# A selective scan's product with C moved between the half scans of the next group

## The chip, the cores and the metric

The kernel runs on one core of one Trainium2 chip. The metric is the device time of one execution in microseconds (us). The engines are TensorE (PE in the rows; PEld is its weight load), VectorE (DVE), ScalarE (ACT), GpSimd (POOL) and SyncE (SP, which issues the DMAs). Each runs its own instructions in order and waits on semaphores for the others.

## What is computed

The input x is 32 images of 14 x 14 positions and 384 channels. A gated recurrent layer over the 196 positions is added to it, and then a selective scan block. The change touches only the second, whose core is

```
dts = softplus(dt_proj(x_dbl) + bias)            # per direction k (4), channel d (192), position t
h   = h * exp(dts[t] * A[n]) + dts[t] * u[t] * B[n, t]      # state n of 16
y   = sum over n of h[n, t] * C[n, t]            # + D * u
```

scanned over t = 0..195 in four directions (rows, columns, and both backwards). The four results are summed, normalised over the channels, multiplied by silu(z) and projected back.

## The kernel before

The scan part goes over 16 pairs of images (`pair`, the first and the last written out, the 14 between in a loop), in each over four stages `st` (the directions), in each over twelve groups `g`. A group is four sequences of 196 positions on 128 partitions (784 columns) of one or more states; 16 x 4 x 12 = 768 groups. Its tile is one of six buffers, `hb`. For each group:

- POOL (`drive`, L495) writes dt * u * B into `hb`. It waits until the group six back has been summed.
- ACT (`decays`, L980 for groups 0 to 7, L984, two instructions a half, for 8 to 11) writes exp(dt * A) of each half group into one of three PSUM banks (`DEC`). The decay of a half waits for the half scan three back.
- DVE (`scan`, L786 forwards, L789 backwards) runs two half scans in place in `hb`, 392 columns each, and then (`read_out`, L798) multiplies the whole tile by C, which lies spread over the partitions in two PSUM banks.
- PE (`spread`, L1258) writes C of the next group into these banks when the product has been made (`readout_ready`), and then (`reduce`, L1268) adds the tile with an identity matrix to the sums in banks 5 and 6.

Between these, at fixed groups, the queues hold the rest. PE has the projections for the next stages, and for the pair before the centring, variance and out-projection (L1283 to L1289, L1316 to L1323). ACT has the softplus of the next stage, the copies of the sums out of banks 5 and 6 (`drain`, L996, at stages 0 and 2), and for the pair before the copies of the centred values (L1002, stage 0, groups 6 and 8), the logarithm of the variance (L1025, stage 1, groups 6 and 8), an affine step (L1013, stage 2, group 2) and the copies of the result (L1019, stage 2 group 8, stage 3 groups 6 and 8). ACT does these after the decays of the group named. PE makes the values for them in stage 0 at groups 4, 5 and 7, in stage 1 at 5 and 7, in stage 2 at 6, in stage 3 at 4 and 6, each after the sum of the group before. Before the sum of the first group of stages 0 and 2, PE waits for the copies of `drain` (L1340 to L1343), because this sum starts the banks anew.

Of the kernel before, what the change touches and what calls it, by code (L numbers as in the profile page):

```python
# [27 lines left out]
PAIRS = B // 2  # L28
# [3 lines left out]
K4 = 4  # L32
T2 = 2 * T
TC = 3 * T
GRP = 12
# [14 lines left out]
def build(nc, x_seq, x_pair, wx, wh, bx, bh, wp, win, par, xproj, dtproj, wout, out):  # L50
# [6 lines left out]
    with ExitStack() as ctx:  # L57
# [3 lines left out]
        def sem(name):  # L61
            return ctx.enter_context(nc.semaphore(name))
# [71 lines left out]
        def carve(cols):  # L134
# [29 lines left out]
        s = {n: sem(n) for n in (  # L164

            "params_in", "gru_weights_in", "late_weights_in", "dt_w_clear", "xload0", "xload1", "xload2", "xload3",

            "ident0", "ident_ready", "sel_step", "gavg_step", "const_ready", "pad_zero", "d_zero", "setup_step",
            "a_exp", "a_capped", "bias_step", "bcw_step", "centring_step", "skip_step",

            "st_done", "a_gn", "a_g1", "a_g2", "a_std", "a_rstd",

# [35 lines left out]
        def group_aps(g):  # L208

            if g < 8:  # L210
                return (lambda a: a[:, 0:T2].unsqueeze(1).broadcast_to([128, 2, T2]),
                        lambda bank: ps[:, bank:bank + 2, 0:T2],
                        lambda a: a.rearrange("p (m c) -> p m c", m=2))
            return (lambda a: a[:, T2:TC].unsqueeze(1).unsqueeze(1).broadcast_to([128, 2, 2, T]),
                    lambda bank: ps[:, bank:bank + 2, 0:T2].rearrange("p m (q t) -> p m q t", q=2),
                    lambda a: a.rearrange("p (m q t) -> p m q t", m=2, q=2))

        def half_cols(hf):

            return slice(hf * HALF_C, (hf + 1) * HALF_C)  # L220
# [323 lines left out]
        def _(dve):  # L544
# [232 lines left out]
            def scan(st, g, hf, G):  # L777

                q = (st * GRP + g) % RING
                bank = (2 * (st * GRP + g) + hf) % DEC  # L780
                if hf == 0:
                    dve.wait_ge(s["drive_ready"], G + 1)
                dve.wait_ge(s["decay_ready"], G * 2 + (hf + 1))
                h = hb[q][:, half_cols(hf)]
                if KS[st] < 2:
                    dve.tensor_tensor_scan(h, ps[:, bank, 0:HALF_C], h, 0.0, ALU.mult, ALU.add  # L786
                        ).then_inc(s["scan_done"], 1)
                else:
                    dve.tensor_tensor_scan(h[:, ::-1], ps[:, bank, 1:HALF_C + 1][:, ::-1], h[:, ::-1], 0.0, ALU.mult, ALU.add  # L789
                                           ).then_inc(s["scan_done"], 1)  # L790

            def read_out(st, g, G):

                _, bank, view = group_aps(g)
                h = view(hb[(st * GRP + g) % RING])
                dve.wait_ge(s["scan_done"], G * 2 + 2)
                dve.wait_ge(s["c_ready"], G + 1)
                dve.tensor_tensor(h, h, bank(3), ALU.mult).then_inc(s["readout_ready"], 1)  # L798

            def pair(i, head, last):  # L800
                for st in range(K4):
                    for g in range(GRP):
                        G = i * (K4 * GRP) + (st * GRP + g)
                        for hf in range(2):
                            scan(st, g, hf, G)
                        read_out(st, g, G)

            pair(0, True, False)
            with nc.Fori(1, PAIRS - 1, engines=[dve.engine], hint_back_edge=True) as i:
                pair(i, False, False)  # L810
            pair(PAIRS - 1, False, True)


        @block.scalar
        def _(act):
# [123 lines left out]
            def mid_parts(P, st):  # L939
                act.wait_ge(s["resid_ready"], P + 1)  # L940
                act.activation(bcs[st][32:64, :], resid[32:64, :], ACT.Copy).then_inc(s["mid_ready"], 1)
                act.activation(midt[64:96, :], resid[64:96, :], ACT.Copy).then_inc(s["mid_ready"], 1)
# [24 lines left out]
            def decays(P, st, g, hf, H, early=False):  # L967

                k, b = KS[st], st % 2
                bank = (2 * (st * GRP + g) + hf) % DEC  # L970
                lo = 1 if k < 2 else 0
                r = ps[:, bank, 0:HALF_C].rearrange("p (r t) -> p r t", t=T)[:, :, 1:T]
                if (g, hf) == (0, 0):
                    act.wait_ge(s["delta_ready"], P + 1)
                if not early:
                    act.wait_ge(s["scan_done"], H - (DEC - 1))
                if g < 8:
                    src = delta[b][:, 0:T2].rearrange("p (r t) -> p r t", r=2)[:, :, lo:lo + T - 1]
                    c = k * N + 2 * g + hf
                    ins = act.activation(r, src, ACT.Exp, scale=a01[:, c:c + 1], bias=abias01[:, c:c + 1])  # L980
                else:
                    for m in range(2):
                        c = k * N + 4 * (g - 8) + 2 * hf + m
                        ins = act.activation(r[:, m, :], delta[b][:, T2 + lo:T2 + lo + T - 1], ACT.Exp,  # L984
                                             scale=a2[:, c:c + 1], bias=abias2[:, c:c + 1])
                ins.then_inc(s["decay_ready"], 1)

            def drain(i, end):

                act.wait_ge(s["reduced"], i * (K4 * GRP) + (48 if end else 24))  # L990
                for dst, bank, rows in (((y_wh if end else y_hw)[:, 0:T2], 5, 2), ((y_wh if end else y_hw)[:, T2:TC], 6, 1)):
                    src = ps[:, bank, 0:rows * T]
                    if end:
                        dst = dst.rearrange("p (r h w) -> p r h w", h=H, w=W)
                        src = src.rearrange("p (r w h) -> p r h w", w=W, h=H)
                    act.activation(dst, src, ACT.Copy).then_inc(s["y_drained"], 1)  # L996
# [7 lines left out]
            def square(i):  # L1004

                act.wait_ge(s["yc_ready"], i * 2 + 2)
                act.activation(ysq, yc, ACT.Square).then_inc(s["ysq_ready"], 1)
# [24 lines left out]
            def pair(i, head, last):  # L1032
                for st in range(K4):
                    P1, n1, k1 = i * 4 + (st + 1), (st + 1) % K4, KS[(st + 1) % K4]
                    ahead = not (last and st == K4 - 1)
                    for g in range(GRP):
                        for hf in range(2):
                            H = i * (2 * K4 * GRP) + (2 * (st * GRP + g) + hf)
                            if not (head and 2 * (st * GRP + g) + hf < DEC):
                                decays(i * 4 + st, st, g, hf, H)  # L1040
                        if g == 1:
                            if st == 0 and not head:
                                drain(i - 1, True)
                            if st == 2:
                                drain(i, False)
                        if ahead:
                            if g == 2:
                                softplus(P1, k1, 0)
                            if g == 3:
                                mid_parts(P1, n1)  # L1050
                            if g == 4:
                                softplus(P1, k1, 1)
                            if g == 5:
                                series(P1, 0)
                            if g == 6:
                                series(P1, 1)
                        if not head:
                            if (st, g) in ((0, 6), (0, 8)):
                                centred(i - 1, g // 2 - 3)
                            if (st, g) == (0, 9):  # L1060
                                square(i - 1)
                            if (st, g) in ((1, 6), (1, 8)):
                                log_var(i - 1, g // 2 - 3)
                            if (st, g) == (1, 9):
                                rstd(i - 1)
                            if (st, g) == (2, 2):
                                affine(i - 1)
                            if (st, g) in ((2, 8), (3, 6), (3, 8)):
                                result(i - 1, (g // 2 - 2) if st == 3 else 0)
                        if (st, g) == (3, 7) and not last:  # L1070
                            act.wait_ge(s["du_ready"], i * 4 + 4)
                            turn(i + 1)
                        if g == 11 and not (last and st >= 2):
                            read_bc(i * 4 + (st + 2), (st + 2) % K4)
# [392 lines left out]
```

## Time and profile before

| | us |
|---|---|
| median of three runs | 3129.97 (3129.74 to 3130.99) |
| the profiled execution | 3124.29, span 3122.5 |
| DVE busy | 2624.9 (84%) |
| PE busy | 2718.1 (87%) |
| POOL busy | 2142.9 (69%) |
| ACT busy | 1812.7 (58%) |

The recurrent layer fills the first third of the span, then come the input projections and the convolution; the scan part runs from about 967 us to 3092 us, with a tail of 30 us. In the rows the first number of a timeline is the start in us from the start of the span, the second how long it lasts, x2 how many instructions are merged in the row; in brackets stands how long the engine was idle before, and who ended that.

### The profile page before, as it was taken

The numbers are of one execution on the slowest core, as the hardware profiler recorded it, in microseconds if no ns is written. First come the engines' busy times: TensorE is split into PE (matmuls) and PEld (weight loads), VectorE is DVE, ScalarE is ACT, GpSimd is POOL, SyncE is SP. The second block draws the span as 40 slices with busy tenths as digits, with TensorE's granted clock in tenths as the row PEclk, the third lists the DMA queues.
The fourth block names the chain that finished last, engine by engine and source line by source line (L and its number), as shares of the span: only waits on it lengthen the run. The fifth ranks groups of instructions, "written<-read, shape, count | busy, mean of one in ns | idle before, by whom it ended". The sixth has DMA issues, their size and how long they took to land.

```text
span 3122.5 us, 100405 instructions
## 1 busy us (share of the span) xinstructions
PE 2718.1 (87%) x39088; PEld 2026.1 (65%) x39088; DVE 2624.9 (84%) x4163; ACT 1812.7 (58%) x3812; POOL 2142.9 (69%) x1816
## 2 busy tenths in 40 slices
PE   4999999999996788888888888888888888888886
PEld 3999999996654465665655656556566656656554
DVE  6444444445999999999999999999999999999995
ACT  1111111112226777777777777777777777777774
POOL 5333333331006888988889888988989889888883
PEclk9999999999998999999999999999999999999999
DMA  5000000002335455454554555555555555545541
GB/s 207 0 0 0 0 0 0 0 0 82 139 133 176 139 164 179 142 177 145 168 165 149 165 159 164 161 168 156 158 168 151 163 165 150 180 144 172 173 125 48
DMA packets 57087, 385.30 MB, mean 123 GB/s; under 512 B 10100, under 2 KB 15060, under 8 KB 31700
## 3 DMA queue, kind: packets, MB, share of 16 engines
q1 hardware_dynamic: 57044, 384.79, 39.8%
q8 instruction: 20, 0.33, 0.0%
q14 instruction: 23, 0.19, 0.0%
HBM read 352.64 MB, written 32.11 MB: 123 GB/s over the span
## 4 chain that ended last, share of the span: by engine, by line
POOL 35%; issue 28%; PE 26%; DVE 8%; ACT 1%; POOLq 1%; DMA 0%; DVEq 0%; ACTq 0%
POOL arena L495 22%; PE ps L1138 10%; PE ps L1147 10%; PE ps L1179 3%; POOL arena L468 3%; POOL arena L477 3%; POOL arena L482 3%; POOL arena L472 3%; DVE arena L789 2%; DVE arena L786 2%; PE ps L1134 2%; DVE conv_out L202 1%; POOL arena L460 1%; DVE stats L571 1%; POOL arena L455 1%
## 5 line engine op out<-in xcount | busy, mean ns | idle before, releaser
L1268 PE MATMUL ps<-arena,ident 128*128 128x392 f32 (+1 forms) x4096 | 1164.3, 417 | 0.9 <-DVE arena L798 0.9
L980 ACT ACTIVATE ps<-arena,abias,a 128x390 f32<-128x390 f32 x1024 | 688.7, 677 | 306.0 <-DVE arena L789 177.0
L1268 PEld LDWEIGHTS ps<-arena,ident 128*128 128x128 f32 x4096 | 683.3, 191 | 144.3 <-issue 1.3
L798 DVE TENSOR_TENSOR arena<-arena,ps 128x784 f32<-128x784 f32 x768 | 745.6, 971 | 28.0 <-PE ps L1258 1.8
L786 DVE TENSOR_TENSOR_SCAN arena<-ps,arena 128x392 f32<-128x392 f32 x768 | 702.7, 956 | 7.5 <-issue 4.4
L789 DVE TENSOR_TENSOR_SCAN arena<-ps,arena 128x392 f32<-128x392 f32 x768 | 702.7, 957 | 0.0
L1258 PE MATMUL ps<-arena,sel 96*128 96x196 bf16 x3072 | 391.7, 250 | 307.9 <-DVE arena L798 307.4
L1258 PEld LDWEIGHTS ps<-arena,sel 96*128 96x128 bf16 x3072 | 230.4, 98 | 612.4 <-DVE arena L798 578.0
L495 POOL TENSOR_TENSOR arena<-arena 128x784 f32<-128x784 f32 x256 | 474.2, 1852 | 133.2 <-PE ps L1268 130.8
L984 ACT ACTIVATE ps<-arena,abias,a 128x195 f32<-128x195 f32 x1024 | 474.6, 504 | 136.3 <-DVE arena L786 69.3
L495 POOL TENSOR_TENSOR arena<-arena,wh_sb 128x784 f32<-128x784 f32 x256 | 472.7, 1852 | 71.8 <-PE ps L1268 69.7
L495 POOL TENSOR_TENSOR arena<-arena,wx_sb 128x784 f32<-128x784 f32 x256 | 466.6, 1856 | 19.5 <-POOL arena L482 15.1
L426 POOL COPY arena<-h_t 128x96 f32 x196 | 71.9, 367 | 407.5 <-DVE h_t L673 407.5
L1138 PE MATMUL ps<-wx_sb,x_cur 128*32 128x96 f32 x14112 | 333.2, 248 | 0.0
L1147 PE MATMUL ps<-wh_sb,h_t 128*32 128x96 f32 x14112 | 332.9, 247 | 0.0
L658 DVE TENSOR_TENSOR rh<-r_gate,ps 128x96 f32<-128x96 f32 x196 | 49.8, 254 | 313.3 <-PE ps L1147 313.3
L1138 PEld LDWEIGHTS ps<-wx_sb,x_cur 128*32 128x32 f32 x14112 | 290.9, 110 | 23.1 <-issue 0.2
L1147 PEld LDWEIGHTS ps<-wh_sb,h_t 128*32 128x32 f32 x14112 | 299.2, 110 | 7.4
L844 ACT ACTIVATE r_gate<-ps 128x96 f32<-128x96 f32 x196 | 49.2, 251 | 399.2 <-PE ps L1147 399.2
L1237 PE MATMUL ps<-arena,bc_w 128*128 128x196 f32 x768 | 149.5, 332 | 2.6 <-DVE gsum L732 2.6
L443 POOL TENSOR_TENSOR grstd<-gsum,neg_half 128x2 f32<-128x2 f32 x16 | 13.5, 844 | 199.3 <-DVE gsum L732 199.3
L1237 PEld LDWEIGHTS ps<-arena,bc_w 128*128 128x128 f32 x768 | 133.2, 192 | 20.2 <-issue 3.0
(180 smaller groups left out, 3025.9 us busy)
## 6 DMA issues: line engine op xcount, KB each, us to landing
wx_sb<-b_by_state SPq DMA_DIRECT2D x64, 1568.0 KB, 6.3
wh_sb<-b_by_state SPq DMA_DIRECT2D x64, 1568.0 KB, 6.3
arena<-b_by_image SPq DMA_DIRECT2D x128, 784.0 KB, 9.0
arena<-x_seq SPq DMA_DIRECT2D x4, 2352.0 KB, 16.1
x_in<-x_pair SPq DMA_DIRECT2D x16, 588.0 KB, 4.2
x_dram<-x SPq DMA_DIRECT2D x16, 588.0 KB, 3.1
x<-x_dram SPq DMA_DIRECT2D x16, 588.0 KB, 10.0
out<-xhat SPq DMA_DIRECT2D x16, 588.0 KB, 2.9
```

Of the source, the lines that this page charges most:

```text
L468: pool.tensor_tensor(rest, soft, rest, ALU.subtract).then_inc(s["rest_ready"], 1)
L495: pool.tensor_tensor(view(hb[(st * GRP + g) % RING]), dux(du[b]), view(src), ALU.mult).then_inc(s["drive_ready"], 1)
L786: dve.tensor_tensor_scan(h, ps[:, bank, 0:HALF_C], h, 0.0, ALU.mult, ALU.add).then_inc(s["scan_done"], 1)
L789: dve.tensor_tensor_scan(h[:, ::-1], ps[:, bank, 1:HALF_C + 1][:, ::-1], h[:, ::-1], 0.0, ALU.mult, ALU.add).then_inc(s["scan_done"], 1)
L798: dve.tensor_tensor(h, h, bank(3), ALU.mult).then_inc(s["readout_ready"], 1)
L980: ins = act.activation(r, src, ACT.Exp, scale=a01[:, c:c + 1], bias=abias01[:, c:c + 1])
L984: ins = act.activation(r[:, m, :], delta[b][:, T2 + lo:T2 + lo + T - 1], ACT.Exp, scale=a2[:, c:c + 1], bias=abias2[:, c:c + 1])
L1138: mm = pe.matmul(ps[32 * j:32 * j + 32, bank + p, 0:CJ], x_cur[:, p, 32 * k:32 * k + 32], wx_sb[:, k, j, lo:lo + CJ], start=False, stop=False)
L1147: mm = pe.matmul(ps[32 * j:32 * j + 32, bank + p, at:at + CJ], h_t[:, 1 - p, 32 * k:32 * k + 32], wh_sb[:, k, j, lo:lo + CJ], start=False, ...
L1237: mm = pe.matmul(ps[:, 7, bc * T:(bc + 1) * T], bc_w[:, k, bc, tile, :], x[:, tile * T:(tile + 1) * T], start=(tile == 0), stop=(tile == 2))
L1258: mm = pe.matmul(ps[:, 3 + m // 2, m % 2 * T:m % 2 * T + T], sel[:, n, kind, :], rhs, start=True, stop=True)
L1268: mm = pe.matmul(ps[:, 5 if g < 8 else 6, 0:cols], ident[:, :], h[:, m * cols:(m + 1) * cols], start=(opens and m == 0), stop=(closes and ...
```

## The change

The product of a group is issued after the first half scan of the next group, so that DVE's order is first half scan of g, product of g-1, second half scan of g. The last product of all stands behind the last pair. It waits for `2 * done` half scans and `done` spreads of C, where `done` is the count of groups before g. On ACT, the copies of the sums (`drain`) go from behind the decays of group 1 to behind those of group 2, in stages 0 and 2. The number of instructions of each engine stays the same.

```diff
-            def read_out(st, g, G):
+            def read_out(st, g, done):
 
                 _, bank, view = group_aps(g)
                 h = view(hb[(st * GRP + g) % RING])
-                dve.wait_ge(s["scan_done"], G * 2 + 2)
-                dve.wait_ge(s["c_ready"], G + 1)
+                dve.wait_ge(s["scan_done"], done * 2)
+                dve.wait_ge(s["c_ready"], done)
                 dve.tensor_tensor(h, h, bank(3), ALU.mult).then_inc(s["readout_ready"], 1)
 
             def pair(i, head, last):
                 for st in range(K4):
                     for g in range(GRP):
                         G = i * (K4 * GRP) + (st * GRP + g)
-                        for hf in range(2):
-                            scan(st, g, hf, G)
-                        read_out(st, g, G)
+                        scan(st, g, 0, G)
+                        if not (head and (st, g) == (0, 0)):
+                            read_out(*((st, g - 1) if g else ((st - 1) % K4, GRP - 1)), G)
+                        scan(st, g, 1, G)
...
             pair(PAIRS - 1, False, True)
+            read_out(K4 - 1, GRP - 1, PAIRS * K4 * GRP)
...
-                        if g == 1:
+                        if g == 2:
                             if st == 0 and not head:
                                 drain(i - 1, True)
                             if st == 2:
```

## Rows read from the trace of the kernel before

**Rows 1.** Costliest groups of the page: busy and mean ns of one; idle before.

```profile
L798 DVE TENSOR_TENSOR arena<-arena,ps 128x784 f32<-128x784 f32 x768 | 745.6, 971 | 28.0 <-PE ps L1258 1.8
L786 DVE TENSOR_TENSOR_SCAN arena<-ps,arena 128x392 f32<-128x392 f32 x768 | 702.7, 956 | 7.5 <-issue 4.4
L789 DVE TENSOR_TENSOR_SCAN arena<-ps,arena 128x392 f32<-128x392 f32 x768 | 702.7, 957 | 0.0
```

**Rows 2.** Windows view, one pair: length; busy PE, PEld, DVE, ACT, POOL; clock, DMA.

```profile
1497.20:1629.30 132.10, 113.86 (x584) 79.81 (x584) 130.46 (x145) 100.11 (x192) 117.37 (x75) 1.00 0.52 160
```

**Rows 3.** Timeline of DVE in that pair, stages 0, 1 and 2.

```profile
1499.09 0.97 DVE L798 TENSOR_TENSOR arena<-arena,ps 128x784 f32<-128x784 f32 x1
1499.98 1.83 DVE L786 TENSOR_TENSOR_SCAN arena<-ps,arena 128x392 f32<-128x392 f32 x2
...
1507.34 0.97 DVE L798 TENSOR_TENSOR arena<-arena,ps 128x784 f32<-128x784 f32 x1
...
1515.60 0.97 DVE L798 TENSOR_TENSOR arena<-arena,ps 128x784 f32<-128x784 f32 x1
...
1530.25 1.83 DVE L789 TENSOR_TENSOR_SCAN arena<-ps,arena 128x392 f32<-128x392 f32 x2
...
1543.12 0.97 DVE L798 TENSOR_TENSOR arena<-arena,ps 128x784 f32<-128x784 f32 x1
...
1548.62 0.97 DVE L798 TENSOR_TENSOR arena<-arena,ps 128x784 f32<-128x784 f32 x1
...
1578.90 0.97 DVE L798 TENSOR_TENSOR arena<-arena,ps 128x784 f32<-128x784 f32 x1
```

**Rows 4.** Timeline of ACT, stage 0, groups 6 to 9.

```profile
1514.60 0.50 ACT L1002 ACTIVATE arena<-ps 128x392 f32<-128x392 f32 x1 [0.59 <-PE ps L1285]
1514.99 1.27 ACT L980 ACTIVATE ps<-arena,abias,a 128x390 f32<-128x390 f32 x2
...
1520.51 0.34 ACT L1002 ACTIVATE arena<-ps 128x196 f32<-128x196 f32 x1 [2.07 <-PE ps L1289]
1520.74 1.82 ACT L984 ACTIVATE ps<-arena,abias,a 128x195 f32<-128x195 f32 x4
```

**Rows 5.** Timeline of PE, stage 0, the spread for group 7.

```profile
1516.63 0.51 PE L1258 MATMUL ps<-arena,sel 96*128 96x196 bf16 x4 [0.39 <-DVE arena L798]
```

**Rows 6.** Timeline of ACT, stage 1, groups 6 to 9.

```profile
1547.36 0.50 ACT L1025 ACTIVATE arena<-ps 128x392 f32<-128x392 f32 x1 [0.33 <-PE ps L1285]
1547.76 1.27 ACT L980 ACTIVATE ps<-arena,abias,a 128x390 f32<-128x390 f32 x2
...
1552.54 0.34 ACT L1025 ACTIVATE arena<-ps 128x196 f32<-128x196 f32 x1 [1.07 <-PE ps L1289]
1552.77 1.82 ACT L984 ACTIVATE ps<-arena,abias,a 128x195 f32<-128x195 f32 x4
```

**Rows 7.** Timeline of ACT, stage 2, groups 1 to 3.

```profile
1565.32 0.72 ACT L996 ACTIVATE arena<-ps 128x392 f32<-128x392 f32 x2 [0.36 <-PE ps L1268]
...
1567.03 0.68 ACT L980 ACTIVATE ps<-arena,abias,a 128x390 f32<-128x390 f32 x1 [0.42 <-DVE arena L786]
...
1569.64 1.27 ACT L980 ACTIVATE ps<-arena,abias,a 128x390 f32<-128x390 f32 x2
```

**Rows 8.** Timeline of all engines at the start of the last pair.

```profile
2961.04 1.28 ACT L980 ACTIVATE ps<-arena,abias,a 128x390 f32<-128x390 f32 x2
...
2961.82 1.84 DVE L786 TENSOR_TENSOR_SCAN arena<-ps,arena 128x392 f32<-128x392 f32 x2 [3.05 <-ACT ps L980]
```

**Rows 9.** Timeline of PE, stage 2: a spread, the out-projection's last.

```profile
1563.41 0.51 PE L1258 MATMUL ps<-arena,sel 96*128 96x196 bf16 x4 [0.89 <-DVE arena L798]
...
1582.94 0.82 PE L1323 MATMUL ps<-x,ident 128*128 128x392 f32 x2
```

**Rows 10.** Timeline of POOL, stage 0: group 10, then the next stage's groups.

```profile
1513.32 1.86 POOL L495 TENSOR_TENSOR arena<-arena 128x784 f32<-128x784 f32 x1 [1.16 <-PE ps L1268]
...
1523.18 7.29 POOL L495 TENSOR_TENSOR arena<-arena,wx_sb 128x784 f32<-128x784 f32 x4 [0.24 <-POOL arena L482]
```

## What the change should do to the time

> **What bounds the kernel now.** I read the costliest groups of instructions first, then the busy time of each engine over one pair of images, then the timelines of VectorE (DVE), ScalarE (ACT) and TensorE (PE). The last 2120 us are 768 groups, each two half scans (L786 or L789) and one product with C (L798) on DVE [rows 1]. Over the 48 groups of the pair from 1497.2 to 1629.3, DVE is busy 130.46 of 132.10 us and no other engine comes near; PE's clock is 1.00, that is 2.4 GHz [rows 2]. So DVE sets the end, and what counts is the distance between the starts of its instructions. One group takes 132.10 / 48 = 2.752 us; its busy time is 130.46 / 48 = 2.718, so 0.034 us is idle.
>
> The durations overlap: 0.956 + 0.957 + 0.971 = 2.884 us [rows 1] against 2.718 covered, so 0.166 us is covered twice. In [rows 3] the product starts at 1499.09 and the next scan at 1499.98, 0.89 later, though the product lasts 0.97; two scans together span 1.83. These two starts overlap what stands before them by 0.166 / 2 = 0.083 us. The third, from the second half scan to the product of the same group, doesn't: the product reads what that scan wrote, waits for its end and starts 0.034 after it. In start-to-start distances: product to scan 0.888, scan to scan 0.873, scan to its own product 2.752 - 0.888 - 0.873 = 0.991.
>
> **What the change removes.** The product of group g-1 now follows the first half scan of g, and what it waits for ended a whole instruction earlier. It should start like any other, 0.873 after the scan ahead of it. The trace has no scan followed by a product that is free to start; the nearest rows are scan to scan and product to scan. A group then takes 0.873 + 0.888 + 0.873 = 2.634 us, 0.118 less, and 768 x 0.118 = 90.6 us is the gain. Its lower bound is the idle time alone, 768 x 0.034 = 26 us, or nothing; I see no reason for more than 0.118. I take 0.118, because both kinds of neighbour in the trace that wait for no DVE result overlap alike.
>
> The Trainium skill ("VectorE: DVE Perf Modes", "The DRAIN you can't avoid") speaks against this: it says that the next operation can't start until the pipe is empty, that a semaphore after each operation costs nothing extra, and in its rules for authors to save operations, not semaphores. The trace's 0.991 against 0.873 is after a wait on DVE's own result and without one. By the page the sum would have no gain term; this is the third rival.
>
> **What it costs: PE's work slides against ACT's.** PE starts group g+1 (C's spread, L1258, then the sum of group g, L1268, then whatever stands behind) when product g is done. ACT's decays (L980, L984) go by the scans. The product now ends one scan later relative to the scans, so wherever ACT waits in its queue for PE, the decays behind that copy come later, and the next scan needs them. ACT has such waits at four places of each pair but the first, at the norm of the pair before: L1002 in stage 0 (groups 6 and 8) and L1025 in stage 1 (groups 6 and 8). Each holds the first decays of group 7 or 9.
>
> I take the length of each chain from the start of the product that releases PE to the end of the decay, plus 0.10 from an ACT end to DVE's start (the decay from 2961.04 ends at about 2961.72, the scan starts at 2961.82) [rows 8]:
> - Stage 0, group 9. Product 6 starts 1515.60 [rows 3], PE's spread 1516.63 [rows 5], the copy 1520.51, the decays 1520.74, two of them done at +0.94 [rows 4]: 1521.68 - 1515.60 + 0.10 = 6.18 us.
> - Stage 0, group 7. Product 3 at 1507.34, copy at 1514.60 after the centring in two groups, decay from 1514.99 (+0.68): 8.43 us [rows 3, 4].
> - Stage 1, group 7. Product 4 at 1543.12, decay from 1547.76 (+0.68): 5.42 us [rows 3, 6].
> - Stage 1, group 9. Product 6 at 1548.62, decays from 1552.77 (+0.94): 5.19 us [rows 3, 6].
>
> The time that DVE gives them was 2 x 2.752 + 0.888 = 6.39 us from product g to the first scan of g+3 (one group more, 9.14, for the second). All four fitted, the first with 0.2 to spare, and DVE doesn't stop there. After the change the product stands behind the first half scan of the next group: the distance is 2 x 2.634 - 0.873 = 4.40 us, or 7.03 with a group more. The stalls are 6.18 - 4.40 = 1.78, 8.43 - 7.03 = 1.40, 5.42 - 4.40 = 1.02 and 5.19 - 4.40 = 0.79, in sum 4.99 us a pair. They add up, since each chain starts from a product behind the stall before it. Fifteen pairs have them: 75 us. With 0.1 us more or less in each of the four, 69 to 81.
>
> **The moved copies** (L996, at stages 0 and 2). They wait for the sum of the last group of the stage before, which also comes a scan later; at group 1 ACT would stand before them, at group 2 it needn't. They start at 1565.32, 1.91 after the spread at 1563.41 [rows 7, 9]; by the new distances that is 3.8 us into the stage, and ACT is through with the decays of group 2 at 4.3. Moved, they stand between the decays of groups 2 and 3. In stage 2, the fullest, ACT goes without rest from the decay at 1567.03 to that of group 3 at 1569.64 [rows 7]. With 0.72 for the copies, and 0.06 from a DVE end to the start that it releases (product 6 ends at 1516.57, the spread starts at 1516.63): 0.06 + 2.61 + 0.72 + 0.68 + 0.10 = 4.17 us, against 2 x 2.634 - 0.956 = 4.31 that DVE gives. It fits by 0.14; nothing is lost, and if it didn't fit, 0.1 us would be lost once a pair. PE waits for them ahead of the sum of the stage's first group (L1343), perhaps 0.2 us; only the spread of group 2 is behind, and between two products it has 2.634 - 0.971 - 0.06 - 0.51 - 0.10 = 1.0 us to spare. No DMA moves.
>
> **Others.** The out-projection's copies (L1019) stand one group further behind PE: product 5 at 1578.90, last matmul from 1582.94 (+0.82) [rows 3, 9]; with 0.50 for the copy (as L1002's of the same shape), 0.94 and 0.10 that is 6.4 us against 7.03. No stall, cover 0.6. GpSimd (POOL) waits for the sum of group 4 before its drive of group 10 [rows 10]. Product g stands at 1.87 + 2.752g of a stage, and at 3.51 + 2.634g after the change, 1.2 us later for group 4, and POOL's work behind it as well. Its drives for the next stage start at 1523.18, 7.29 / 4 = 1.82 each: the first is done 5.2 us before its scan at 1530.25 [rows 3]. That leaves 5.2 - 1.2 - 12 x 0.118 = 2.6 us: covered. The last product stands at the end of the queue as before; the tail doesn't change.
>
> **Sum.** -90.6 + 75 = -15.7 us. The profiled execution took 3124.29 us (span 3122.5), so it would be 3108.6; the median of the runs shown is 3129.97, 5.7 more, and from it the forecast is 3114.3.
>
> **Rivals.**
> 1. *The stalls outweigh the gain* (slower). The point from which it decides is 90.6 / 15 = 6.04 us a pair, one more than my sum. It comes where a cover that I call sufficient isn't: 0.1 at the moved copies, 0.6 at the out-projection's copies, or PE a little later at the four. For it: the covers are small and ACT is busy 100.11 of 132.10 us [rows 2]. With 6.8 us a pair it is +11 us, 3141 us. Against it: the chains are measured whole, not put together. Chance 0.15.
> 2. *The chains are shorter than counted*, because a part of PE's work that I hang on the product can run before it. With 3 us a pair: 3130 - 90.6 + 45 = 3084 us. For it: group 7 of stage 0 hangs on three groups of PE's queue. Against it: the spread stands first in each group of that queue and waits for the product. Chance 0.14.
> 3. *DVE starts no product until the scan before it has ended.* Then the change doesn't do what it says. If only the 0.034 goes, a group takes 2.718, the distances are 4.48 and 7.20, the stalls 4.58 a pair: 3130 - 26 + 69 = 3173 us, chance 0.06. If nothing goes: distances 2 x 2.752 - 0.991 = 4.51 and 7.27, stalls 4.42: 3130 + 66 = 3196 us, chance 0.03. Against both: the 0.083 at the other two starts.
>
> **How the numbers follow.** Forecast 3114 us, chance 0.62, its own range 3102 to 3129 (stalls 69 to 81, gain per group 0.113 to 0.120, and 5 us either way for the last pair, where DVE stands 3.05 us for ACT [rows 8]). Range for 8 in 10: from rival 2 to rival 1, 3084 to 3141; left out are 0.09 of rival 3 and tails. A measurement here can tell some 0.2% from nothing, 6.3 us: faster below 3123.7. Of the forecast's 0.62 some 0.53 lies there, with rival 2 0.67; 0.12 within; 0.21 slower, from rivals 1 and 3.
>
> **What will show it.** The start distances on DVE: first half scan to product 0.87 (rival 3: 0.96 or more), a group in stages 2 and 3 at 2.63 us, 31.6 us for twelve. DVE's idle time before a scan with ACT's L980 and L984 as releasers, some 75 us in all, 1.4 and 1.8 us at groups 7 and 9 of stage 0, 1.0 and 0.8 in stage 1; none in the first pair. ACT's waits for PE at L1002 and L1025 grow by about 2 us each. Stalls at group 3, or in stages 2 and 3, would mean that a cover failed (rival 1). The prediction is wrong if stages 0 and 1 take as long as 2 and 3.

## The result, and the profile after

The changed kernel takes 3090.62 us (median; 3084.21 to 3094.28), the kernel before beside it 3130.48 us: a ratio of 0.987 (95% interval 0.9853 to 0.9887), 39.9 us faster. The forecast was 3114.3 us. The time lies inside the stated range and on the forecast side, but below the forecast's own range of 3102 to 3129, and the gain is 2.5 times the 15.7 us that the sum gave. The profiled execution took 3084.21 us, 40.1 less than that of before, so the two profiles show the whole difference.

The costliest groups of the page after, which answer [rows 1] (busy and mean ns of one, then idle before and its main releaser):

```profile
L786 DVE TENSOR_TENSOR_SCAN arena<-ps,arena 128x392 f32<-128x392 f32 x768 | 708.9, 958 | 44.6 <-ACT ps L986 24.9
L789 DVE TENSOR_TENSOR_SCAN arena<-ps,arena 128x392 f32<-128x392 f32 x768 | 708.8, 958 | 23.3 <-ACT ps L982 13.3
L798 DVE TENSOR_TENSOR arena<-arena,ps 128x784 f32<-128x784 f32 x768 | 727.2, 947 | 1.0 <-PE ps L1260 0.6
```

The 28.0 us that DVE idled in front of products are 1.0; in front of scans it idles 67.9 us, released by ACT's decays (L982 and L986 are the lines L980 and L984 of before). The product itself is shorter, 947 ns against 971. The timeline of DVE in stage 0 of a pair, groups 6 to 9, which answers [rows 3]:

```profile
1501.71 0.97 DVE L786 TENSOR_TENSOR_SCAN arena<-ps,arena 128x392 f32<-128x392 f32 x1 [1.28 <-ACT ps L982]
1502.60 0.94 DVE L798 TENSOR_TENSOR arena<-arena,ps 128x784 f32<-128x784 f32 x1
1503.47 1.83 DVE L786 TENSOR_TENSOR_SCAN arena<-ps,arena 128x392 f32<-128x392 f32 x2
1505.21 0.94 DVE L798 TENSOR_TENSOR arena<-arena,ps 128x784 f32<-128x784 f32 x1
1506.08 0.97 DVE L786 TENSOR_TENSOR_SCAN arena<-ps,arena 128x392 f32<-128x392 f32 x1
1508.70 0.97 DVE L786 TENSOR_TENSOR_SCAN arena<-ps,arena 128x392 f32<-128x392 f32 x1 [1.66 <-ACT ps L986]
1509.59 0.94 DVE L798 TENSOR_TENSOR arena<-arena,ps 128x784 f32<-128x784 f32 x1
```

A group without a stall goes from product to product in 1505.21 - 1502.60 = 2.61 us: product to scan 0.87 (1502.60 to 1503.47), two scans to the next product 1.74. In medians over all groups of the two traces, the three distances between starts went so: from a product to the scan behind it 0.888 before and 0.863 after, from that scan to the next one 0.883 and 0.883, from the second scan to the product 0.981 and 0.865. ACT in the same stretch, which answers [rows 4]:

```profile
1500.61 0.50 ACT L1004 ACTIVATE arena<-ps 128x392 f32<-128x392 f32 x1 [2.47 <-PE ps L1287]
1501.01 1.27 ACT L982 ACTIVATE ps<-arena,abias,a 128x390 f32<-128x390 f32 x2
...
1507.49 0.34 ACT L1004 ACTIVATE arena<-ps 128x196 f32<-128x196 f32 x1 [3.45 <-PE ps L1291]
1507.72 1.82 ACT L986 ACTIVATE ps<-arena,abias,a 128x195 f32<-128x195 f32 x4
```

ACT waits 2.47 and 3.45 us for PE where it waited 0.59 and 2.07; the decays behind each copy release the stalled scans. In the rows of DVE a stall shows as 1.28 and 1.66 us of idle time, but it costs 1.38 and 1.77: the scan also lasts 0.97 us where one right behind another scan lasts 0.95, and it can't overlap what stands ahead.

**Where the 40.1 us are.** Times go from product start to product start. The last row is what the others leave over; in it, the stretch ahead of the first scan, on which the change has no part, took 965.1 us after and 967.5 before.

| | before | after | difference, us |
|---|---|---|---|
| a group without a stall | 2.752 | 2.610 | 768 x -0.142 = -109.1 |
| pair in the loop, 48 groups | 132.11 | 130.52 | |
| of it over 48 groups at that rate (stalls) | 0 | 5.24 | 15 x 5.24 = +78.6 |
| what the first 12 groups of the last pair take over those of a loop pair | 8.1 | 0.5 | -7.6 |
| rest (ahead of the scans, first pair, tail) | | | -2 |

### The profile page after: what moved, and what is told of

Its sections match the earlier page's. It is cut to its first block, busy times and chain, and to the rows that moved or that the text cites. A ratio compares the mean times of both kernels' runs of the same rounds, so it can differ in the third digit from the quotient of the medians.

```text
span 3082.4 us, 100405 instructions
## 1 busy us (share of the span) xinstructions
PE 2710.2 (88%) x39088; PEld 2029.7 (66%) x39088; DVE 2553.4 (83%) x4163; ACT 1813.3 (59%) x3812; POOL 2143.2 (70%) x1816
## 4 chain that ended last, share of the span: by engine, by line
POOL 36%; PE 28%; issue 26%; DVE 8%; ACT 1%; POOLq 1%; DMA 0%; DVEq 0%; ACTq 0%
POOL arena L495 22%; PE ps L1140 10%; PE ps L1149 10%; PE ps L1181 3%; POOL arena L468 3%; POOL arena L472 3%; POOL arena L477 3%; POOL arena L482 3%; PE ps L1136 2%; DVE arena L789 1%; DVE arena L786 1%; DVE arena L798 1%; POOL arena L460 1%; DVE conv_out L202 1%; POOL arena L455 1%
## 5 line engine op out<-in xcount | busy, mean ns | idle before, releaser
L1270 PE MATMUL ps<-arena,ident 128*128 128x392 f32 (+1 forms) x4096 | 1164.1, 417 | 0.0
L982 ACT ACTIVATE ps<-arena,abias,a 128x390 f32<-128x390 f32 x1024 | 684.6, 678 | 208.3 <-DVE arena L789 109.8
L1270 PEld LDWEIGHTS ps<-arena,ident 128*128 128x128 f32 x4096 | 681.6, 190 | 149.5 <-ACT arena L998 6.5
L798 DVE TENSOR_TENSOR arena<-arena,ps 128x784 f32<-128x784 f32 x768 | 727.2, 947 | 1.0 <-PE ps L1260 0.6
L1260 PEld LDWEIGHTS ps<-arena,sel 96*128 96x128 bf16 x3072 | 237.9, 97 | 566.8 <-DVE arena L798 529.3
L986 ACT ACTIVATE ps<-arena,abias,a 128x195 f32<-128x195 f32 x1024 | 465.9, 503 | 54.5 <-DVE arena L786 34.1
L495 POOL TENSOR_TENSOR arena<-arena,wx_sb 128x784 f32<-128x784 f32 x256 | 467.2, 1854 | 24.8 <-PE ps L1270 15.7
```

Of the source, the lines that this page charges most:

```text
L495: pool.tensor_tensor(view(hb[(st * GRP + g) % RING]), dux(du[b]), view(src), ALU.mult).then_inc(s["drive_ready"], 1)
L1260: mm = pe.matmul(ps[:, 3 + m // 2, m % 2 * T:m % 2 * T + T], sel[:, n, kind, :], rhs, start=True, stop=True)
L1270: mm = pe.matmul(ps[:, 5 if g < 8 else 6, 0:cols], ident[:, :], h[:, m * cols:(m + 1) * cols], start=(opens and m == 0), stop=(closes and ...
```

## The experiments

The theory after the result: a DVE instruction that waits for the end of the one right ahead of it pays 0.142 us for that, not the 0.118 of the forecast, and the stalls come from ACT's queue order as forecast. Rivals: the product is faster by where it stands; the stalls are a lack of time that would only move; the moved copies carry a part of the gain. Each kernel below was timed beside the kernel before, on the same chip as the others of its group.

### The two parts alone

Only the moved copies, in the old order:

```diff
-                        if g == 1:
+                        if g == 2:
                             if st == 0 and not head:
                                 drain(i - 1, True)
```

> The old order on DVE, only the copies of the sums (drain) moved on ACT from group 1 to group 2. Theory (all of the gain comes from DVE's order): the same time as before, within 3 us; a group stays at 2.752 us, no idle time of DVE in front of a scan in the loop. Rival (the moved copies carry a part of the gain that the rate of the scans doesn't explain): faster by 5 us or more.

Measured: 3153.53 us against 3130.14, ratio 1.007 (1.0054 to 1.0087), 23 us slower. Neither theory had this. The waits of the kernel (in all, times, longest), the timeline of PE at the start of one stage 0, and a row from the stage 2 behind it:

```profile
DVE arena L798 <- PE ps L1258: 23.5, 28, 1.5
PE ps L1268 <- ACT arena L996: 53.4, 31, 1.7
```

```profile
1510.40 0.51 PE L1258 MATMUL ps<-arena,sel 96*128 96x196 bf16 x4 [0.23 <-DVE arena L798]
...
1512.64 2.44 PE L1268 MATMUL ps<-arena,ident 128*128 128x392 f32 x4 [1.72 <-ACT arena L996]
1514.87 0.86 PE L1258 MATMUL ps<-arena,sel 96*128 96x196 bf16 x4
...
1579.79 1.58 PE L1268 MATMUL ps<-arena,ident 128*128 128x392 f32 x4 [1.72 <-ACT arena L996]
```

PE stands 1.72 us for the copies before it may start the banks anew, and then, in the first of the two stages, runs for the most part at the lower of its two clocks: the sum takes 2.44 us where it took 1.51, the spread of C 0.86 for 0.51. The windows view (length; busy PE, PEld, DVE, ACT, POOL; granted clock, DMA share, GB/s) has 0.61 of full speed for that stretch, a mean of times at 1.2 and at 2.4 GHz, and 1.00 before it:

```profile
1508.00:1512.60 4.60, 2.68 (x16) 1.82 (x14) 4.53 (x6) 2.70 (x6) 4.50 (x4) 1.00 0.45 174
1512.60:1515.40 2.80, 2.76 (x8) 1.46 (x9) 2.25 (x3) 2.75 (x6) 0.25 (x1) 0.61 0.95 390
```

The product of group 2 then waits 0.98 us for C. The trace tells the wait from the clock, since PE stands the same 1.72 us at all 31 of these places. Behind 13 of them, as at 1579.79, the sum took 1.58 or 1.59 us and the products lost 0.01 us or nothing. Behind the other 18 PE ran slowly (the sum 1.90 to 2.98 us) and the products lost 1.06 to 1.46 us each, but for one that lies among the gaps of the last pair: in sum some 20 of the 23 us. So in the old order the late copies do harm, not by PE's wait itself, but by the clock that falls behind some of the waits.

Only the new order of DVE, the copies left at group 1 (the last hunk of the change undone):

> The new order on DVE with the copies of the sums left at group 1. ACT then stands at group 1 until the sum of the last group of the stage before, about 3.8 us into the stage. Theory: in stage 2, where softplus and the affine step follow, the decay of group 3 is done 8.4 us into the stage and the scan wants it at 7.83: 0.6 us of DVE idle once a pair, 9 us in all, about 3099 us. Rival (the place of the copies doesn't matter): 3090 us, no idle time at group 3.

Measured: 3097.03 us, ratio 0.9894 (0.9877 to 0.991), as expected within 2 us. The stall is in front of the scan of group 3 in stage 2, as expected, and 0.38 us long where 0.6 was worked out:

```profile
1563.44 0.97 DVE L786 TENSOR_TENSOR_SCAN arena<-ps,arena 128x392 f32<-128x392 f32 x1 [0.38 <-ACT ps L982]
```

The order alone is worth 33 us. The copies give another 6.4 on top of it, and cost 23 without it: the two parts belong together.

### What a wait for the instruction ahead costs

The changed kernel, where the product waits for one half scan more, the one right ahead of it, which it doesn't read (`own` is 1, and 0 for the very last product):

```diff
-                dve.wait_ge(s["scan_done"], done * 2)
+                dve.wait_ge(s["scan_done"], done * 2 + own)
```

> The new order, but the product also waits for the half scan right ahead of it, whose result it doesn't read. Theory A (a DVE instruction that waits for the end of the one ahead pays for it, wherever it stands: 0.034 idle, 0.083 of overlap, and 0.024 by which it lasts longer itself): product 0.971 long again, a group 2.752 us, the four stalls 4.4 us a pair: about 3130 + 66 = 3196 us, less some 7 if the last pair's gap stays away. Theory B (the product is short because of where it stands beside PE's work): product 0.945, a group 2.728 or less, under 3180 us.

Measured: 3183.63 us against 3130.14, ratio 1.0169 (1.0152 to 1.0186), 93 us slower than the changed kernel by one wait. The timeline of DVE:

```profile
1567.19 0.97 DVE L798 TENSOR_TENSOR arena<-arena,ps 128x784 f32<-128x784 f32 x1
1568.07 1.83 DVE L789 TENSOR_TENSOR_SCAN arena<-ps,arena 128x392 f32<-128x392 f32 x2
1569.94 0.97 DVE L798 TENSOR_TENSOR arena<-arena,ps 128x784 f32<-128x784 f32 x1
```

The product is 0.97 long again and a group takes 2.75 us, in the new place. That is theory A. The stalls of a loop pair are 136.39 - 132.11 = 4.28 us, the third rival's second case gave 4.42 for this rate. So 768 waits cost 109 us at 0.142 each, and some 14 of them come back as smaller stalls (4.28 us a pair for 5.24); the total of 3183.63 is 5 us under the 3189 that theory A gave without the last pair's gap. The same wait for another engine does the same to the length: 16 products of the changed kernel waited for C until 0.02 us after the end of the scan ahead, and they last 0.971 too.

The product behind both half scans of the next group, so that it waits for nothing near, with ACT's norm steps moved as in the next section:

```diff
                         scan(st, g, 0, G)
+                        scan(st, g, 1, G)
                         if not (head and (st, g) == (0, 0)):
                             read_out(*((st, g - 1) if g else ((st - 1) % K4, GRP - 1)), G)
-                        scan(st, g, 1, G)
```

> As e4 (ACT's norm steps one group later), but the product of the group before stands behind both half scans of the next group, not between them. It waits for no DVE result that isn't long there. Theory (what counts is that the product doesn't wait for the instruction ahead; the place is free): product 0.945 us, a group 2.610 us in stages without a stall, as between the halves. The product comes 0.87 us later, so PE's chains end later: from product 6 to the scan of group 10 there are 6.1 us against 6.2, at the out-projection 6.1 against 6.4; some 1 us a pair of stalls, 3040 us. Rival (it must stand between the halves, since two scans side by side and the product behind them cost more): a group over 2.65 us, over 3060 us.

Measured: 3038.74 us against 3129.11, ratio 0.9713 (0.9697 to 0.973). Its rate is the same:

```profile
1576.67 0.94 DVE L798 TENSOR_TENSOR arena<-arena,ps 128x784 f32<-128x784 f32 x1
1577.54 1.83 DVE L789 TENSOR_TENSOR_SCAN arena<-ps,arena 128x392 f32<-128x392 f32 x2
1579.29 0.94 DVE L798 TENSOR_TENSOR arena<-arena,ps 128x784 f32<-128x784 f32 x1
```

So the place between the half scans isn't what matters for the rate; it is only the earliest one that doesn't wait. The later place costs 15.5 us against the next kernel, which has the product between the halves. A pair takes 126.87 us, 0.94 more, about the 1 us that was expected, but not where it was expected: the scan that idles is that of group 3 in stage 2, 0.64 us each time.

### Where the stalls come from

The changed kernel, ACT's copies of the centred values and the logarithms (and the square and rstd behind them) one group later:

```diff
-                            if (st, g) in ((0, 6), (0, 8)):
+                            if (st, g) in ((0, 7), (0, 9)):
                                 centred(i - 1, g // 2 - 3)
-                            if (st, g) == (0, 9):
+                            if (st, g) == (0, 10):
                                 square(i - 1)
-                            if (st, g) in ((1, 6), (1, 8)):
+                            if (st, g) in ((1, 7), (1, 9)):
                                 log_var(i - 1, g // 2 - 3)
-                            if (st, g) == (1, 9):
+                            if (st, g) == (1, 10):
                                 rstd(i - 1)
```

> The new order, and on ACT the copies of the centred values, their square, the logarithms of the variance and the rstd one group later (stage 0 at groups 7, 9, 10; stage 1 the same). Theory (the four stalls a pair come from the decays that stand behind these copies in ACT's queue): the idle time of DVE in front of scans goes from about 68 us to under 5, a pair in the loop takes 125.5 us instead of 130.5, the total is 3090 - 73 = 3017 us. Rival (the stalls are a lack of time on ACT or PE and only move): the idle time comes back at groups 8 and 10, and the total stays over 3070 us.

Measured: 3023.22 us (3022.80 to 3027.33) against 3130.14, ratio 0.9661 (0.9645 to 0.9677). This version beats both kernels, the changed one by 67 us, and is 6 us behind what was expected. The groups of its page and a window of its scan part:

```profile
L786 DVE TENSOR_TENSOR_SCAN arena<-ps,arena 128x392 f32<-128x392 f32 x768 | 709.8, 967 | 0.4 <-ACT ps L982 0.4
L789 DVE TENSOR_TENSOR_SCAN arena<-ps,arena 128x392 f32<-128x392 f32 x768 | 708.1, 963 | 0.0
```

```profile
1497.20:1629.30 132.10, 119.29 (x623) 85.94 (x622) 132.08 (x152) 105.02 (x202) 122.89 (x79) 1.00 0.57 169
```

Of the 67.9 us of idle in front of scans 0.4 is left, and DVE is busy 132.08 of 132.10 us. A pair takes 125.93 us, not 125.5; that is the 6 us. What it has over 48 x 2.610 = 125.28 are mostly steps of 2.68 to 2.71 us at groups where the product comes just behind C.

Stage 0's steps alone, stage 1 left:

> The changed kernel with only stage 0's norm steps of ACT one group later; stage 1's logarithms stay. Theory (each stall belongs to its own copy, and they add up): stage 0 loses its 1.39 + 1.77 us, stage 1 keeps 1.00 + 0.77: 3090 - 15 x 3.0 = 3045 us. Rival (the stalls are one lack that moves on): stage 1's stalls grow, the total stays over 3060 us.

Measured: 3046.23 us, ratio 0.974 (0.9724 to 0.9756). In stage 1 the distances from product to product stay 3.60 and 3.38 us, as in the changed kernel. The stalls belong each to its own copy.

The same move of ACT's steps in the old order:

> The old order on DVE (copies of the sums at group 1, as before), and only ACT's copies of the centred values, the square, the logarithms and the rstd one group later. In the old order these stop no scan. Theory (moving them gives back stalls of the new order, and nothing else): the same as before, 3130 us within 3. Rival (their early place costs something in the old order too): faster by 5 us or more. Second reading: the last pair's gap on DVE in front of the scan of group 9 of stage 0, 4.4 us in the profile of before and not there in any kernel with the new order; if the old order's code brings it, it is here again.

Measured: 3128.75 us against 3129.11, ratio 1.0001 (0.9991 to 1.001). By itself it does nothing: the old order has no such stalls, and a pair in its loop takes 132.1 us with the move and without it.

### PE standing before the sums

The changed kernel with the copies of the sums at group 3 (`g == 3` for `g == 2`):

> The changed kernel with the copies of the sums one group later still, at group 3. PE then stands before the sum of group 0 until they are through, from 4.9 to about 7.6 us into stages 0 and 2, as it stood 1.7 us in the old order with the copies at group 2. The spread of C for group 2 comes behind that sum, and the product of group 2 would start at 8.7. Theory A (PE's granted clock falls after it has stood, so that the sum takes 2.4 us and not 1.35, as in the old order): the product of group 2 starts 1.9 us late, twice a pair, 60 us in all, about 3150 us, and the windows view shows a clock well under 1.00 there. Theory B (PE only stood, at its full clock): 0.85 us late, 27 us, about 3117 us.

Measured: 3178.94 us against 3130.22, ratio 1.0156 (1.0139 to 1.0173). Its waits, and one stage 0:

```profile
DVE arena L798 <- PE ps L1260: 84.2, 51, 3.4
PE ps L1270 <- ACT arena L998: 93.2, 31, 3.5
```

```profile
1514.85 2.36 PE L1270 MATMUL ps<-arena,ident 128*128 128x392 f32 x4 [2.59 <-ACT arena L998]
1585.60 1.58 PE L1270 MATMUL ps<-arena,ident 128*128 128x392 f32 x4 [3.40 <-ACT arena L998]
```

In the first row PE stood 2.59 us and ran slowly behind it (granted clock 0.69 from 1514 to 1518), in the second it stood 3.40 us and the sum went at nearly full speed. Of the 31 places of this kind 24 are slow behind the wait (the sum takes 1.91 to 2.98 us) and 7, all in stage 2, are not (1.58 or 1.59). The products lose 2.3 to 4.3 us at each of the 24, and 1.7 or 1.8 at each of the 7. So both theories have a part: the clock falls at most of the places, as theory A has it, but the wait alone costs 1.7 us where PE stood 3.4, twice what theory B gave it. Together they make 88 us where theory A had 60. What decides whether the clock falls, neither this run nor the one with the old order tells. In the changed kernel the matmuls of the sums have no idle time ahead of them at all (0.0 in the page's group L1270).

### The last pair's gaps

DVE stands twice in front of a scan at the start of the last pair of the kernel before, and once more, 0.5 us, in front of a product. The waits of DVE there ("issue": nothing that the profile shows), of before and then of the changed kernel:

```profile
DVE arena L786 <- issue: 4.4, 1, 4.4
DVE arena L786 <- ACT ps L980: 3.1, 1, 3.1
```

```profile
DVE arena L786 <- ACT ps L982: 1.7, 2, 1.3
DVE arena L786 <- ACT ps L986: 1.7, 1, 1.7
```

Of these rows of the changed kernel only 0.4 us is the gap of before, the rest are the known stalls. Three kernels asked whether the place of the instructions decides. The first was meant to put eight waits ahead of DVE's scan part:

> The kernel before with eight waits on a value long reached, on DVE ahead of the scan part: they take nothing worth measuring, but every DVE instruction behind them lies eight places further on. Theory A (the last pair's gap in front of group 9, 4.4 us without a waited-for event, comes from where the instructions lie): it moves to another group or goes, and the time may fall by up to 5 us. Theory B (it comes from the order of the work or the traffic at that moment): the gap stays in front of group 9 of stage 0 with 4 us or more, and the time is that of before.

Measured: 3128.27 us against 3129.11, ratio 1.0004 (0.9994 to 1.0013), with a gap of 7.7 us in front of group 9. The waits moved the code by fewer places than was meant. Three semaphore instructions of the new line stand in the trace, and a fourth at L782; they hold one or two waits each, and the rest hang on instructions that were there. The first lines of the two pages, of before and of this run, differ by those four:

```profile
span 3122.5 us, 100405 instructions
span 3125.6 us, 100409 instructions
```

So four places further on, the gap is still in front of group 9. The next two use small memsets, one in the new order (shown) and 16 in the old:

```diff
+            for n in range(1):
+                dve.memset(gru_bias[:, n:n + 1], 0.0).then_inc(s["const_ready"], 1)
             pair(0, True, False)
```

> The changed kernel with one small memset more on DVE ahead of the scan part. In the changed kernel the first pair has one instruction less than before, so that DVE's loop and last pair lie one place earlier; the memset puts them back to the places they have in the kernel before. Theory A (the last pair's gap of 4 to 7 us on DVE in front of the scan of group 9 hangs on where the instructions lie): the gap is there again, and the median is 3095 us or more. Theory B (it hangs on the order): no gap in front of group 9, 3090.6 us within 3.

> The kernel before with 16 small memsets more on DVE ahead of the scan part (1 to 2 us by themselves), so that its loop and last pair lie 16 places further. Theory A (place): the gap in the last pair moves to another group or goes; where it goes the time is 3130 + 2 - 6 = 3126 us. Theory B (order): the gap stays in front of group 9, 3132 us.

Measured: 3091.08 us for the new order (the changed kernel: 3090.62), with no gap in front of group 9; 3127.63 us against 3131.13 for the old, ratio 0.9992 (0.9982 to 1.0001), where the gap in front of group 9 is gone and one of 1.74 us stands in front of group 7:

```profile
2975.87 1.27 ACT L982 ACTIVATE ps<-arena,abias,a 128x390 f32<-128x390 f32 x2
...
2977.08 0.94 ACT L986 ACTIVATE ps<-arena,abias,a 128x195 f32<-128x195 f32 x2
...
2978.61 1.84 DVE L786 TENSOR_TENSOR_SCAN arena<-ps,arena 128x392 f32<-128x392 f32 x2 [1.74 <-ACT ps L986]
```

The releaser named can't be the true one: L986 (L984 of before) makes group 8's decays, and those of group 7, L982 here, end at 2977.14, 1.5 us before the scan. It is a gap of the same kind, two groups earlier.

Counting all of DVE's instructions in the trace, those of its sequencer too, the gap stands in front of number 8124 in the kernel before (and in those with the moved copies and with ACT's steps later), of 8128 with the eight waits and of 8130 with the 16 memsets. In the old order it keeps to nearly the same place in the code, whatever the group, 1.7 to 7.7 us long. The new order shows none, with or without the memset, but the old place isn't quite met there: by the same count its last pair begins four instructions earlier than before, and three earlier with the memset. The kernel with the product behind both half scans has a small one, 0.9 us, in front of number 8122 and of group 9. So the place decides where the gap stands, and the order has a part in whether there is one.

The trace also has the packets that load instruction code, as a kind of their own. From 1200 to 2940 us, within the loop, the kernel before has none. Its last pair is straight code that runs for the first time, and in the first 50 us of it there are seven. One of them lies in the gap of DVE, between 2980.4 and 2981.2 us. In the run with the 16 memsets one lies in the gap in front of group 7, between 2976.8 and 2977.2. The DMA view of these two windows (queue and kind, packets, MB, share of 16 engines; the data packets have the first row):

```profile
q1 hardware_dynamic: 16, 0.20, 125.6%
q14 instruction: 1, 0.01, 5.0%
```

```profile
q14 instruction: 1, 0.01, 5.3%
```

In all six programs with such a gap (the five of the old order and the one with the product behind both half scans) a packet of code ends 1.3 to 1.7 us before DVE goes on. ACT's stop at the start of the last pair, 5.2 us in the kernel before and 1.7 in the changed one, has one too, and ACT goes on 1.2 and 1.3 us after its end. In the changed kernel the packet ends 26.5 us after the loop, and the scan of group 9, in front of which the gap would stand, starts at 29.6; in the kernel before it ends at 31.5, and DVE has stood since 28.8. So the likely cause is that the engine waits for its code. It is not shown: the trace doesn't say whose code a packet holds. Why the packet comes 5 us later in one order than in the other stays open; while DVE stood in the kernel before, data packets filled the DMA engines (the first fence), and in the short gap with the 16 memsets there were none.

## Why the prediction was wrong in size

- **DVE sets the end, one rate for all groups, the first 0.118 of the gain**: right. The overlap of 0.083 and the idle 0.034 came back as read. The distance into the product fell by 0.116 (0.981 to 0.865). The prediction had 0.991 and 0.873, since it took the mean length of a scan, 0.956, for each; a scan lasts 0.966 behind a product and 0.947 behind a scan. The two errors cancel in the sum.
- **The gain per group** is the step that failed. It was 0.142 us, not 0.118: 18.4 us over 768 groups. I took product to scan, 0.888, as a constant. It contains the product's own length, and a product that has waited for the end of the scan ahead lasts 0.971, one that hasn't 0.945 (0.94 in the rows above). The scan behind it starts 0.025 sooner (0.863 for 0.888). These 18.4 us are more than the whole forecast gain of 15.7, which was the small difference of two large terms, 90.6 and 75. "I see no reason for more than 0.118" was the wrong sentence: every product of the trace of before had waited, so its length was measured only in that condition. The scans of the same trace show that a length depends on what stands ahead, 0.947 or 0.966, and the upper bound should have been open by about that much. The changed kernel and the one with the added wait have the same order of work, and the product lasts 0.945 in the one and 0.971 in the other.
- **The four stalls**: right, and the closeness is in part luck. Forecast 1.40, 1.78, 1.02 and 0.79 us at groups 7, 9, 7, 9; the steps from product to product are 3.99, 4.38, 3.60 and 3.38 us, over 2.61 by 1.38, 1.77, 0.99 and 0.77, in sum 4.91 against 4.99. In the same order the four chains, from product to scan, are 8.33, 6.10, 5.32 and 5.10 us, each 0.08 to 0.10 shorter than counted. The time that DVE gives them is 6.97 for the first and 4.36 for the others, shorter by 0.06 and 0.04. The two errors pull opposite ways. The small steps in stages 2 and 3 that I put at nothing are 0.33 us a pair, 5 us in all.
- **The moved copies**: right that they cost nothing in the new order. That PE's wait for them costs little I had taken from the length of the wait alone. In the old order and at group 3 PE's clock also fell behind 18 and 24 of 31 such waits.
- **The last pair**: 7.6 us of gain that I had in the range as 5 either way, not in the sum. I had no mechanism for it; that DVE waits there for its code is likely, and not shown.
- **The third rival**, with the page's rule (the Trainium skill, "VectorE: DVE Perf Modes", "The DRAIN you can't avoid": a semaphore after each operation costs nothing extra), fell: one such wait on each of 768 products costs 93 us here. The same section also says that a next operation that is not held starts earlier, which the overlap of 0.083 agrees with; the prediction left this out. Rival 1 fell with the stalls at 5.24 us a pair, under its 6.04; rival 2 fell, as the chains are 0.35 us a pair shorter than counted, not the 2 us that it needs. The wide range held the result by its lower end, 3084, which came from this rival: luck, since its mechanism had no part.

With the measured terms the sum is -109.1 + 78.6 - 7.6 - 2 = -40.1 us, where the 2 is what is left over. Of the difference to the forecast's -15.7, 18.4 us is the product's length and 7.6 the last pair; the stalls, with the small steps, took 3.6 back.

## What to carry to other kernels

On an engine that is always busy, look at which instructions wait for the result of the one right ahead, and put one independent instruction between: here the price of such a wait was 0.034 us of idle time, 0.083 of lost overlap and 0.025 of a longer instruction, and only the first shows as idle. Where this moves an instruction behind others, follow every queue that hangs on it, and move what waits in those queues by the same step; here that was worth more than the change itself. A duration from a trace in which every instance has waited is not the duration without the wait.

## What the runs showed of the hardware

- A DVE product of 784 columns lasts 0.971 us if it waited for the end of the scan ahead, 0.945 if not; start to start the wait costs 0.142 us in all, in two places of the order alike.
- After PE had stood 1.72 us for ACT, its granted clock was 0.61 in the next 2.8 us, and a sum of 1.51 us took 2.44. It was not so each time: of 31 waits of this same length, 18 were followed by a slow sum and 13 by one of 1.58 us. With the copies at group 3, where PE stood 2.6 to 3.5 us, 24 of 31 were followed by a slow sum.
- In the first groups of straight code behind the loop, ACT and DVE stood up to 5.2 and 7.7 us without an event. In the old order the gap of DVE keeps to the same stretch of the code (numbers 8124 to 8130 of its instructions in three placements), and a packet that loads code ended 1.3 to 1.7 us before DVE went on, in six programs of six.
